# Channel attention on one core: V and M two slots later, the early statistics behind the last result block, and the last pair's V two blocks later

## The reference

```python
x = x + conv(group_norm(x, G=32))        # x: (16, 192, 48, 48) f32

def conv(x, w_qkv, temperature, w_out, b_out):      # heads 8, d = 24, n = 48*48 = 2304
    xt = x.reshape(b, c, n).transpose(0, 2, 1)
    q, k, v = jnp.split(xt @ w_qkv, 3, axis=-1)      # each reshaped to heads
    q = q / max(sqrt(sum(q * q over n)), EPS);  k = k / max(sqrt(sum(k * k over n)), EPS);  k = k * temperature
    attn = softmax(einsum('bhpn,bhnq->bhpq', k, q))  # 24 x 24 for each head
    out = einsum('bhnp,bhpq->bhnq', v, attn)
    return (out.reshape(b, n, c) @ w_out + b_out), back to (b, c, 48, 48)
```

## Time and profile before

| | |
|---|---|
| median of 3 runs | 395.95 us (395.7 to 397.17) |
| the profiled execution | 396.41 us, its span 394.6 us |
| PE busy | 334.6 us, 85% of the span |
| DVE busy | 286.3 us, 73% |
| ACT busy | 234.8 us, 59% |
| POOL busy | 148.5 us, 38% |
| mean DMA rate | 172 GB/s |

### The profile page before, as it was taken

How to read it: one execution, slowest core, us unless ns; L and a number is a source line. 1 busy time by engine, 2 the same in 40 slices (tenths; PEclk the granted TensorE clock), 3 DMA queues, 4 the chain that set the end, 5 groups by cost and what they waited for, 6 DMA issues and landing times.

```text
span 394.6 us, 9324 instructions
## 1 busy us (share of the span) xinstructions
PE 334.6 (85%) x3724; PEld 232.2 (59%) x3724; DVE 286.3 (73%) x668; ACT 234.8 (59%) x409; POOL 148.5 (38%) x131
## 2 busy tenths in 40 slices
PE   0068476999789999899989988999989998997795
PEld 0056245775568576766677556756676577763453
DVE  5987777776697679776987659867977665359564
ACT  1098299646876398637875587638874697610200
POOL 0179458204670177115830367016820494001000
PEclk9999858999999999999999999999999999999899
DMA  8999700015992299525980498327961562044556
GB/s 249 358 280 251 172 0 2 2 42 129 312 288 76 84 284 323 152 81 154 320 287 7 156 311 264 109 82 220 328 214 42 160 216 68 2 135 141 176 189 199
DMA packets 30826, 67.73 MB, mean 172 GB/s; under 512 B 5504, under 2 KB 12096, under 8 KB 30784
## 3 DMA queue, kind: packets, MB, share of 16 engines
q1 hardware_dynamic: 30544, 66.56, 53.9%
q10 hardware_dynamic: 240, 0.59, 0.6%
HBM read 29.38 MB, written 28.31 MB: 146 GB/s over the span
## 4 chain that ended last, share of the span: by engine, by line
PE 49%; DVE 15%; ACT 12%; issue 11%; DMA 8%; POOL 2%; SPq 2%; ACTq 0%; POOLq 0%
PE u_ps L891 21%; PE g_ps L891 14%; DMA x_sb<-in_x_dram 8%; PE s_ps L891 8%; ACT tok L550 4%; DVE bnst L694 3%; ACT h_sb L525 2%; ACT h_sb L532 2%; DVE x_sb L818 2%; ACT xn L519 2%; PE u_ps L940 2%; PE u_ps L941 2%; DVE n L736 1%; DVE s_ps L771 1%; DVE ax L773 1%
## 5 line engine op out<-in xcount | busy, mean ns | idle before, releaser
L456 POOL TENSOR_TENSOR l_sb<-xn,h_sb 128x768 f16<-128x768 f32 x63 | 103.6, 1650 | 54.6 <-ACT h_sb L525 54.4
L818 DVE SCALAR_TENSOR_TENSOR x_sb<-u_ps,bias,x_sb 128x384 f32<-128x384 f32 x144 | 85.9, 613 | 28.6 <-PE u_ps L891 28.6
L891 PE MATMUL g_ps<-tok 128*128 128x64 f16 (+1 forms) x864 | 86.2, 240 | 4.4 <-ACT tok L550 4.3
L694 DVE BATCH_NORM_STATS2 bnst<-x_sb 128x6 f32<-128x384 f32 x144 | 70.7, 545 | 16.7 <-DMA x_sb<-in_x_dram 16.5
L519 ACT ACTIVATE xn<-x_sb,rb 128x768 f32<-128x768 f32 x63 | 63.6, 1020 | 31.7 <-POOL rb L468 31.7
L550 ACT COPY tok<-u_ps 128x384 f32<-128x384 f32 x144 | 64.8, 484 | 25.9 <-PE u_ps L943 25.6
L891 PE MATMUL u_ps<-h_sb,ml 128*128 128x384 f16 (+1 forms) x336 | 73.7, 329 | 0.0
L891 PEld LDWEIGHTS g_ps<-tok 128*128 128x128 f16 x864 | 56.6, 99 | 29.2 <-ACT tok L550 6.8
L525 ACT ACTIVATE h_sb<-x_sb,rb 128x768 f16<-128x768 f32 x63 | 64.4, 1022 | 0.0
L891 PE MATMUL u_ps<-hl,mh 128*128 128x384 f16 (+1 forms) x192 | 48.3, 338 | 6.9 <-DVE x_sb L818 6.9
L940 PE MATMUL u_ps<-id,h_sb 128*128 128x128 f16 x288 | 48.6, 222 | 5.5 <-DVE l_sb L684 5.5
(11 more groups left out here) (142 smaller groups left out, 567.7 us busy)
## 6 DMA issues: line engine op xcount, KB each, us to landing
x_sb<-in_x_dram SPq DMA_DIRECT2D x48, 384.0 KB, 5.2
out_dram<-x_sb SPq DMA_DIRECT2D x48, 384.0 KB, 2.9
out_dram<-x_sb SPq DMA_DIRECT2D x48, 192.0 KB, 2.8
x_sb<-in_x_dram SPq DMA_DIRECT2D x45, 192.0 KB, 5.3
hl<-h_sb SPq DMA_DIRECT2D x48, 96.0 KB, 2.8
hl<-l_sb SPq DMA_DIRECT2D x48, 96.0 KB, 2.9
x_sb<-in_x_dram ACTq DMA_DIRECT2D x3, 192.0 KB, 4.3
w<-in_L_conv_w_qkv_dram SPq DMA_DIRECT2D x1, 288.0 KB
```

Of the source, the lines that this page charges most:

```text
L456: nc.gpsimd.tensor_tensor(l_sb[:, par, t, cols], xn[:, c % XN_RING, :], h_sb[:, par, t, cols], ALU.subtract).then_inc(l_ok, 1)
L694: ins = V.bn_stats(bnst[:, t, 6 * part:6 * part + 6], xcol(q, t, part * BW, BW))
L818: V.scalar_tensor_tensor(out=xs, in0=block_ps(n), scalar=bias[:, t:t + 1], in1=xs, op0=ALU.add, op1=ALU.add).then_inc(out_ok, 1)
L891: return nc.tensor.matmul(dst, lhs, rhs, start=start, stop=stop, skip_group_check=True)
```

## The change

On TensorE V moves from behind slot 6 to behind slot 8, and M from behind slot 9 to behind slot 11. ScalarE's casts of both move by the same two slots, from behind copy 9 of `tok` to behind copy 11, and from behind copy 12 to behind copy 14. VectorE's `v` and `m` keep their keys in `VEC_A`. The early statistics go from six to four pieces; the four that stood behind result block 12, ahead of `norms`, are now behind block 17 and `spread`, in place of the two there. The two pieces given up go to phase A (14 instead of 12). In the first step's table two pieces instead of six stand ahead of `norms`, and two behind `spread`. In the last tables, V moves from behind block 14 to behind block 16.

```diff
-PE_A = {0: ["flip"], 6: ["v"], 9: ["m"]}
+PE_A = {0: ["flip"], 8: ["v"], 11: ["m"]}
...
-BN_EARLY = 6
+BN_EARLY = 4
...
-LAST_PE_B = {0: ["gram"], 2: ["w0"], 3: ["w1"], 5: ["scores"], 10: ["flip"], 14: ["v"]}
+LAST_PE_B = {0: ["gram"], 2: ["w0"], 3: ["w1"], 5: ["scores"], 10: ["flip"], 16: ["v"]}
```

More of the change, by code:

```diff
@@ L53 @@
 G_C, G_HL, G_B = 192, 256, 448
-PE_A = {0: ["flip"], 6: ["v"], 9: ["m"]}
+PE_A = {0: ["flip"], 8: ["v"], 11: ["m"]}
 PE_B = {0: ["gram"], 2: ["sums"], 4: ["w0"], 6: ["w1"], 12: ["scores"]}
-ACT_A = {0: ["h6"], 2: ["h7"], 4: ["x8"], 6: ["exp", "h8"], 9: ["v"], 12: ["m"]}
+ACT_A = {0: ["h6"], 2: ["h7"], 4: ["x8"], 6: ["exp", "h8"], 11: ["v"], 14: ["m"]}
 ACT_B = ["x0", "t0", "t1", "t2", "h0", 1, 2, 3, 4, 5, "x6", "x7"]
@@ L74 @@
 VEC_A = {0: ["soft_in"], 3: ["soft_out"], 7: ["v"], 11: ["m"], 17: ["stats"]}
-VEC_B = {0: ["gram"], 2: ["var"], 4: ["z"], 6: ["t0", "t1", "t2"], 12: ["bn", "bn", "bn", "bn", "norms"], 17: ["spread", "bn", "bn"]}
+VEC_B = {0: ["gram"], 2: ["var"], 4: ["z"], 6: ["t0", "t1", "t2"], 12: ["norms"], 17: ["spread", "bn", "bn", "bn", "bn"]}
 FIRST_PE_A = {14: ["wv"]}
@@ L83 @@
 FIRST_VEC_A = {17: ["bn"] * 10 + ["wv"] + ["bn"] * 4 + ["stats", "low0", "low1"]}
-FIRST_VEC_B = {0: ["var", "gram", "z", "low2", "low3", "t0", "t1"], 1: ["t2", "bn", "bn", "bn", "bn", "low4", "low5", "bn", "bn",
-                                                                        "norms", "spread"]}
-BN_A = {1: 2, 5: 3, 9: 4, 13: 3}
-BN_EARLY = 6
+FIRST_VEC_B = {0: ["var", "gram", "z", "low2", "low3", "t0", "t1"], 1: ["t2", "bn", "bn", "low4", "low5", "norms", "spread", "bn", "bn"]}
+BN_A = {1: 2, 5: 4, 9: 4, 13: 4}
+BN_EARLY = 4
 POOL_SECONDS = (3, 5)
 LAST_PE_A = {0: ["m"]}
-LAST_PE_B = {0: ["gram"], 2: ["w0"], 3: ["w1"], 5: ["scores"], 10: ["flip"], 14: ["v"]}
+LAST_PE_B = {0: ["gram"], 2: ["w0"], 3: ["w1"], 5: ["scores"], 10: ["flip"], 16: ["v"]}
 LAST_ACT_A = {0: ["m"]}
```

## The result

The changed kernel takes 383.86 us in the median (383.51 to 384.88, 4 runs), beside 396.56 us for the kernel before in the same measurement. The ratio of the two is 0.9684, with a 95% interval of 0.9637 to 0.973: 3.2% faster. The forecast was 377.6 us, so two thirds of the forecast gain came, about 12.7 of 18.3 us. The time lies outside the forecast's own 374.5 to 381 and inside the stated range, 374.8 to 386, which took in two rivals. The profiled execution has a span of 381.7 us, where the earlier trace rows is of one of 394.6.

The account below looks back on a forecast made before the run. TensorE's list bounds steps 0 to 6, with waits ahead of V and block 17. Terms 6.9 + 7.5 + 1.5 + 2.4 = 18.3 us off 395.95 give 377.6; own range 374.5 to 381, stated range 374.8 to 386.

Parts of the forecast that it names:

- two rivals: VectorE takes over the bound (chance 0.22, 384.8 us) and the stall on loads moves into phase A (0.08, 384.5 us).
- Block 17: TensorE's wait for VectorE ahead of result block 17, steps 0 to 4, goes with the pieces off block 12: 6.9 us.
- V in the middle steps: TensorE's 1.33 us wait for `ax` ahead of V goes: 1.25 for each of steps 1 to 6, 7.5 us.
- The four banks hold that.: VectorE about 1.4 us late for block 0 costs nothing; without the margin, up to 1.4 a step is given back.
- The idle ahead of `z`: VectorE's 1.36 us idle there was to make good its lateness at block 0, leaving the wait near zero.
- the signs named for being wrong: TensorE waiting for VectorE in blocks 4 to 8, or for `ax` over 0.5, or phase A pieces waiting for loads.
- VectorE takes over the bound: Rival, chance 0.22: `ax` 0.5 late and half of block 0's 1.4 not made good, 7.2 us lost: 384.8.
- Step 0: First step: norms start 0.7 us earlier; `flip`'s 0.63 and V's 0.94 waits go, less 0.1: 1.5 us.
- Step 7: Last pair: V's wait falls from 2.70 to about 1.0, M starts earlier; 2.4 us, between 1.9 and 2.6 by clock.
- stall into phase A: Rival, chance 0.08: phase A pieces wait for loads and block 17's gain is given back as late block 0: 384.5.
- No change: Rival, chance 0.03: V's and block 17's waits are replaced in full by `ax` and GpSimd's power: 395 to 397 us.
- M too late: Rival, chance 0.04: TensorE stops at slot 15 for `mh` casts and block 0 for `ml`; slower, 402 us.

Follow-up runs that it names:

- e2: Changed kernel with V and M back at their old places, the last pair's too, so only the statistics pieces move: 387.85 us; kernel before 396.98.
- e1: Kernel before with only V and M of the middle steps two slots later on TensorE and ScalarE: 393.54 us; kernel before 396.98.
- e9: e6 with V and M back behind slots 6 and 9 in the middle steps, ScalarE's casts too: 386.63 us, beside 377.61 for e6.
- e6: Changed kernel with the edits of both e4 and e5: 377.85 us (kernel before 398.63); measured again, 377.61 us (kernel before 396.88).
- e4: Changed kernel with VectorE's low half of the Gram matrix behind result block 1 instead of block 0: 380.2 us; kernel before 396.98.
- e5: Changed kernel with one statistics piece moved from behind `ml` to ahead of it: 381.65 us; kernel before 398.63.
- e7: Changed kernel with 3 statistics pieces ahead of `ml` and 5 behind it, instead of 4 and 4: 386.26 us; kernel before 398.63.
- e8: e6 with the last pair's V back behind block 14 instead of 16: 379.59 us, beside 377.61 for e6.
- e3: Kernel before with only the last pair's V behind block 16 instead of 14: 396.02 us; kernel before 396.98, ratio 0.9964.

## Why the prediction was right in its direction and too high in its gain

**Block 17.** Right, and a little under. Its wait is gone in every step. The length of a step between two starts of V gives the term: from 280.10 to 321.68 it is 41.58 now, from 290.03 to 331.75 it was 41.72, in step 5, which had no such wait. That is 0.14 less. The starts of V of steps 1, 2, 5 and 6, now:

```profile
113.81 0.25 PE L890 MATMUL s_ps<-wvh,ax 96*96 96x192 f16 x1
...
155.38 0.25 PE L890 MATMUL s_ps<-wvh,ax 96*96 96x192 f16 x1
...
280.10 0.25 PE L890 MATMUL s_ps<-wvh,ax 96*96 96x192 f16 x1
...
321.68 0.25 PE L890 MATMUL s_ps<-wvh,ax 96*96 96x192 f16 x1
```

and those of steps 1, 5 and 6 before:

```profile
117.53 0.28 PE L891 MATMUL s_ps<-wvh,ax 96*96 96x192 f16 x1 [1.33 <-DVE ax L774]
...
290.03 0.28 PE L891 MATMUL s_ps<-wvh,ax 96*96 96x192 f16 x1 [1.33 <-DVE ax L774]
...
331.75 0.28 PE L891 MATMUL s_ps<-wvh,ax 96*96 96x192 f16 x1 [1.32 <-DVE ax L774]
```

From step 1 to step 2 it is 155.38 - 113.81 = 41.57 for 159.81 - 117.53 = 42.28, 0.71 less. The difference, 0.57, is block 17's in step 1, for 0.36 of idle: some 0.2 more in each of five steps than the idle that the rows show, 7.9 us in all for 6.9. The end of a multiplication is modelled in the trace, which may account for it; no run tested that. e2, where only the pieces moved, has 41.72 or 41.73 in every middle step, and e1, where they stayed, still waits 6.2 us ahead of block 17. So it is the pieces that this term hangs on.

**V in the middle steps.** Right: TensorE's wait for `ax` is gone in steps 0 to 6. The 1.25 a step that was forecast is borne out by the 0.14 of step 5, with the new wait put back: 0.14 + 1.12 = 1.26. e9 and e6 give the same, 1.27.

**"The four banks hold that."** This is the step that failed. VectorE was forecast to be late for block 0 by about 1.4 us, and it is late by 1.47. I looked for whom it keeps waiting in the ring alone, where block 4 needs block 0, and then at `z`. The group sums, behind block 2, need block 1, as `group_sums` says in its second wait; it is a bank shared by two writers, not the ring's own order. With 0.74 us of the Gram half between block 0 and block 1, the lateness arrives there almost whole, and 1.12 x 6 = 6.7 us of the gain go back. The idle ahead of `z`, on which I counted to make it good, lies 4 us further on. e4, e5, e6 and e7 show this link in the size of each part; e2 shows that it needs V's later place, since the same pieces behind an earlier V keep nobody waiting, and e1 that one piece is 0.46 of it. The prediction's sentence "if it were not there, up to 1.4 a step would be given back" has the right size for the wrong place. None of the signs named for being wrong came, since none looked at the sums. The idle ahead of `z`, forecast near zero and measured at 1.36, did tell.

The rival "VectorE takes over the bound" had the same lateness and, at 384.8, a time nearer to the 383.86 than the forecast. That is luck in part: it priced 0.5 a step at `ax`, where no wait came, and 0.7 at `z`, where VectorE was the one that idled.

**Step 0.** Forecast 1.5, measured 2.9: V begins at 72.24, 1.29 earlier than the 73.53 of the earlier trace rows, though two slots (1.57) more lie ahead of it. V's 0.94 went, as forecast, but `flip`'s wait did not: it was 0.60 in the changed kernel, and the one ahead of it, for `tok`, fell by 0.39. The rest is the clock. Busy time by stretch, behind it the granted clock, DMA share and GB/s, changed kernel:

```profile
66.20:69.50 3.30, 3.30 (x52) 2.73 (x51) 3.16 (x8) 3.30 (x8) 3.30 (x3) 1.00 0.01 2
360.00:363.70 3.70, 3.35 (x11) 1.64 (x12) 0.91 (x2) 0.00 (x0) 0.00 (x0) 0.54 0.41 110
```

In the kernel before, the stretch from 66.0 to 69.5 had a granted clock of 0.53. The change's order by itself doesn't bring the full clock: e4, whose lists are the same up to V of step 0, had the half clock there too:

```profile
66.20:69.50 3.30, 3.30 (x30) 2.50 (x27) 3.12 (x8) 2.83 (x5) 3.30 (x3) 0.50 0.01 2
```

Its V began at 73.71. Over the seven profiled executions with these lists (the change, e4 to e8 and e6 again) V began between 72.24 and 74.15, and the change's is the earliest. By e4 the term is 73.53 + 1.57 - 73.71 = 1.4. So the forecast 1.5 was about right, in part through another wait than it named, and the other 1.4 us of the 2.9 is luck of that execution. What sets the clock apart wasn't tried.

**Step 7.** The step up to M was as forecast, and more: M of the last pair starts 2.51 us behind V, for 370.86 - 365.54 = 5.32 before, 2.8 us. Then 1.6 went back: from M to the end of the span it is 381.7 - 356.38 = 25.3 us, and it was 394.6 - 370.86 = 23.7. The second row above shows it. TensorE waits 2.19 us for `ml`, as before, but the granted clock now falls behind that wait, to 0.54, the level of 1.2 GHz, and the first result blocks run at it. In the kernel before it had fallen behind the wait for `ax`, and stayed full behind `ml`. So the step gave 1.2 net in the profiled execution. e3, with this edit alone, shows the same two parts, and e8 takes the edit away at a kernel without other waits and loses 2.0. e4 had no such stretch behind `ml` at all (its granted clock is 1.00 from 355 to 362), with the same instructions in the step; nor had e7. So where the half clock falls is in part chance, and the term lies between 1.2 and 2.8.

By the rule of the Trainium skill, "TensorE: Matmul & The Clock Gate", section "HAM oscillation — how this bites in real kernels", that long idle gaps bring the half clock back, the shorter gap ahead of V would keep the full clock there. The trace agrees: the clock was 1.00 from 354.5 to 358.0. The prediction stopped at that gap. It had no term for a drop behind the next one, the 2.19 us for `ml`, and that is the second step of it that failed, for 1.6 us in this execution.

**The rivals.** Loads did not move their stall into phase A. No change and M too late did not happen: `ml` was ready for block 0 in steps 0 to 6, and in step 7 the wait for it is the 2.19 of before. Of the sum, 18.3 us: block 17 came to 7.9 for 6.9, V in the middle to 1.26 x 6 = 7.6 for 7.5, step 0 to 2.9 for 1.5, step 7 to 1.2 for 2.4, and the wait that was missing to -6.7. That is 12.9, which is 394.6 - 381.7. It is the sum for this pair of executions, with step 0's lucky clock in it. That e6 lands on the forecast is in part chance too: its profiled execution gives 7.9, 7.6, 2.1 and 1.1, where the forecast had 6.9, 7.5, 1.5 and 2.4.

## What to carry to other kernels

When a step is moved later to give its input time, its output has less time by as much. List everyone who waits for the engines behind it, by the waits in the code and not by the buffer ring alone; a small writer that borrows a corner of another's bank is such a wait. If an engine comes out late by a known amount at a place where it had idled before, look for idle ahead of it to put work in and for work that can pass behind the block waited for: here a piece into 0.8 us of idle and one swap of order gave back what the change had lost. What an edit is worth depends on what stands around it: moving V in the middle steps gave 1.27 us a step where the sums didn't wait (e9 to e6), and 0.14 a step where they did (e2 to the change). The gain of the change came nearly all from the pieces and from the two ends of the program.

## What the hardware showed that I had not expected

The granted clock of TensorE fell to half in the last pair of most kernels. The wait for `ax` was 2.70 us in four profiled executions (the kernel before, e1, e2, e8), and it fell behind all four; it was 0.96 or 0.97 in the other eight, and it fell behind none. The wait for `ml` was 2.19 in all twelve, and behind that one it fell in seven and not in five (the kernel before, e1, e2, e4 and e7). In the middle of the program it is as uneven. At block 17 of step 0 it stayed at 1.00 behind a wait of 2.09 in the kernel before and was 0.50 behind one of 2.00 in e1. In the kernel before, a wait of 2.96 us left it at 1.00; in e3, the same program up to there, it fell behind one of 2.44. Busy time by stretch of e3, behind it the granted clock, DMA share and GB/s:

```profile
193.00:196.50 3.50, 3.39 (x25) 2.35 (x26) 3.06 (x7) 0.79 (x2) 3.06 (x3) 0.51 0.72 200
```

The length of a gap by itself doesn't decide it, and each such stretch behind `ml` cost 1.3 to 1.8 us: from the last pair's M to the end of the span it is 23.7 or 23.8 us in the five executions without one, and 25.0 to 25.5 in the seven with one, for the same work.

Idle that the trace shows ahead of a matmul was some 0.2 us less than what its removal gave, in block 17's five waits. Ahead of the sums the two agree, 1.12 shown and 41.58 - 40.45 = 1.13 gained, and ahead of V less came back than was shown, 1.27 of 1.33.
